# Context handed in turned, layer 3's keys and values computed at the end of the first part, layer 2 quantised by GpSimd, layer 1's scores used in PSUM, and a new order of the queues

## The reference

```
x = x + cross_attention_16_heads(norm(x), ctx)      # layer 0, softmax over the queries
x = x + switch_head_attention(norm(x))              # 8 heads, 5 experts, top 2
x = x + topk_attention(norm(x), ctx, 32)            # layer 1
      scores = (q @ k.T) / sqrt(128); the 32 largest of 77 stay; softmax
x = x + gqa_and_experts(norm(x))                    # causal attention, 8 experts, top 2
x = x + softmax(norm(x) @ ctx.T) @ ctx              # layer 2
x = x + quantised_ffn(norm(x))
      s = sigmoid(clip) * max(abs(n)) / 127         # one scale for the whole tensor
      xq = clip(round(n / s), -128, 127) * s        # 128 -> 352, silu(gate) * up,
      h quantised in the same way, 352 -> 128
x = x + causal_cross_attention_16_heads(norm(x), ctx)   # layer 3
x = x + relu(norm(x) @ w1 + b1) @ w2 + b2
```

## Time and profile before

| | us |
|---|---|
| runs of the kernel before | 1615.16, 1619.88, 1623.08; median 1619.88 |
| profiled execution | 1624.02, its span 1622.1 |
| mean granted TensorE clock of that execution | 0.821 |
| busy: TensorE, VectorE, ScalarE, GpSimd | 1231.1, 1072.0, 989.0, 758.4 |
| part A, up to GpSimd's first all-reduce | about 1245 |
| part B, up to the second all-reduce | about 58 |
| part C | about 319 |

### The profile page before, as it was taken

How to read it: one execution, slowest core, us unless ns; L and a number is a source line. 1 busy time by engine, 2 the same in 40 slices (tenths; PEclk the granted TensorE clock), 3 DMA queues, 4 the chain that set the end, 5 groups by cost and what they waited for, 6 DMA issues and landing times. The chain is left out here.

```text
span 1622.1 us, 36294 instructions
## 1 busy us (share of the span) xinstructions
PE 1231.1 (76%) x13755; PEld 920.0 (57%) x13755; DVE 1072.0 (66%) x2499; ACT 989.0 (61%) x3185; POOL 758.4 (47%) x859
## 2 busy tenths in 40 slices
PE   2677877888787897888888898676752558999986
PEld 2566765675664575566666576454431136777764
DVE  3456665788786677886569777755534879855642
ACT  2677778675768778768768866643432334445531
POOL 2038386485882268458245748732110013433431
PEclk9577677889977897997797988688865569999997
DMA  5000000000000000000000000000001100000000
GB/s 143 1 6 1 1 1 1 2 2 1 4 13 1 16 2 2 6 12 1 1 16 2 1 12 1 1 12 1 1 7 48 47 9 7 12 16 9 9 9 14
DMA packets 29637, 18.26 MB, mean 11 GB/s; under 512 B 6456, under 2 KB 27032, under 8 KB 29464
## 3 DMA queue, kind: packets, MB, share of 16 engines
q1 hardware_dynamic: 29464, 15.93, 3.5%
HBM read 11.73 MB, written 4.19 MB: 10 GB/s over the span
## 5 line engine op out<-in xcount | busy, mean ns | idle before, releaser
L1448 DVE TENSOR_REDUCE arena<-pair 128x8 f32<-128x1024 f32 (+2 forms) x224 | 239.7, 1095 | 115.5 <-PE pair L465 49.5
L1019 ACT ACTIVATE arena<-bank 128x512 f32<-128x512 f32 (+5 forms) x352 | 182.0, 540 | 187.1 <-PE bank L417 86.4
L2073 POOL TENSOR_SCALAR_AFFINE_SELECT arena<-arena 128x1024 f32<-128x1024 f32 (+1 forms) x128 | 145.0, 1154 | 287.8 <-ACT arena L1417 145.7
L2111 POOL TENSOR_TENSOR arena<-arena 128x512 f32<-128x512 f32 x160 | 181.3, 1133 | 50.7 <-DVE arena L1565 35.5
L1079 ACT ACTIVATE arena<-pair,arena 77x128 f32<-77x128 f32 x512 | 178.6, 374 | 23.3 <-DVE arena L1448 22.2
L1027 ACT ACTIVATE arena<-arena 128x128 f32<-128x128 f32 x288 | 117.5, 489 | 105.5 <-POOL arena L2084 97.2
L2116 POOL TENSOR_TENSOR arena<-arena 128x512 f32<-128x512 f32 x128 | 175.1, 1368 | 10.0
L417 PE MATMUL bank<-ident,arena 128*128 128x128 f32 (+2 forms) x448 | 85.6, 327 | 120.0 <-ACT arena L1027 62.5
L417 PEld LDWEIGHTS bank<-ident,arena 128*128 128x128 f32 (+2 forms) x448 | 59.2, 171 | 147.4 <-ACT arena L1027 75.1
L2081 POOL TENSOR_SCALAR arena<-arena 128x4 f32<-128x4 f32 x56 | 18.3, 327 | 225.7 <-DVE arena L1455 223.7
L1417 ACT ACTIVATE arena<-pair 77x1024 f32<-77x1024 f32 x64 | 61.8, 1015 | 99.3 <-PE pair L948 99.3
(11 more groups left out here) (255 smaller groups left out, 3001.9 us busy)
## 6 DMA issues: line engine op xcount, KB each, us to landing
arena<-in_ctx SPq DMA_DIRECT2D x24, 154.0 KB
arena<-in_x SPq DMA_DIRECT2D x8, 256.0 KB, 4.6
spill<-arena SPq DMA_DIRECT2D x8, 256.0 KB, 2.1
arena<-spill SPq DMA_DIRECT2D x8, 256.0 KB, 3.7
out<-arena SPq DMA_DIRECT2D x8, 256.0 KB, 2.5
wexp<-in_L_ffn_expert_w SPq DMA_DIRECT2D x1, 512.0 KB, 4.1
arena<-in_L_ffn_w SPq DMA_DIRECT2D x2, 256.0 KB, 3.1
wsq<-in_L_ffn_Wq SPq DMA_DIRECT2D x1, 256.0 KB, 3.1
```

What stands on the lines that cost most here:

```text
L1019: return act.activation(dst, src, func, bias=bias, scale=scale)
L1448: return dve.tensor_reduce(dst, src, X, op, **kw)
L2073: return pool.affine_select(out=e, in_=e, compare_op=ALU.is_ge, fill=0.0, base=0, pattern=[[0, 8], [1, 128]], channel_multiplier=-1)
L2111: pool.tensor_tensor(into, xvs[:, b, ex * SHD:(ex + 1) * SHD].unsqueeze(1).broadcast_to([128, SH, SHD]), gates[g % 2][:, b, 0:SH, ex].unsq ...
```

## The change

- The host hands the context in a second time, turned (in_ctx_turned, channels first). The transposes and the copies of them are gone in all three places; layer 0 loads only the turned one, layers 1 and 2 both. Each turned tile is loaded when its buffer is free.
- Layer 3's keys and values (stream y, kv3) are computed for all eight groups in part A, from one load of the whole turned context and two weights. That load stands in the SP queue behind the spill of group 5 and waits for the last output of layer 0, whose buffers it takes over. The results stay in SBUF (kf3, v3); part C only spreads them.
- Part B's quantisation is done by GpSimd in the same three passes. The memsets of part C's tiles go to GpSimd behind it. An all-reduce whose result isn't used stands ahead of the first one.
- Layer 1's scores aren't copied: the scale goes into the copy of the queries (with a bias scaled once, b1qs), the first round of the top-k and the exponentials read PSUM, and the bank is drained by the exponentials.
- The last sum is written into x and stored from there; y4 is gone.
- GpSimd's norm waits for the apply of its last use.
- All strings of ORDER are new.

```diff
 ORDER = {
     ("A", "tensor"):
-        "aaaiaaiibbwabwwcbwbcbbcbacaacaabbb...
+        "iiawaaabbwbwwcbbcbbcbacaacabbb...
...
-        "...inlhlkmililkimllmiliimmjnjjjnknnlknnllknnmknnllmllnnmlnnmmnnnnnnnnnnnnnnnn"
+        "...iilliinmlliimilyyymyyymiyyiyyiyynynnyyyjjjnnjknnlknnllnnkmllnknmllnnmlnmmnnnnnnnnnnnnnnn"
     ("A", "scalar"):
-        "aaaaiaibbwwawbcwbbcbb...
+        "iaawaawbbwwbcbbcbbc...
     ("A", "vector"):
-        "awwwawibbwwwcbwabbcbb...
+        "awwiwwwaawbbwwbcbbcbb...
     ("B", "vector"):
-        "aabbabbbbabbbbabbbbabbbbabbbbabbbbbbbbbb",
+        "bbbbbbbbbbbbbbbbbbbbbbbbbbbbbbbb",
+    ("B", "gpsimd"):
+        "aaaaaaaa",
...
             def x0p(g):
                 yield
-                pe.wait_ge(ctx0_in, 16 * (g + 1))
-                o = E.take("x0", g, "ctx")
-                pe.wait_ge(o.drained, o.n)
-                transpose4(o, ctx0[0:CTX], CTX).then_inc(o.full, 1)
-                yield
-                c = E["x0", g, "ctx"]
+                pe.wait_ge(ctx0_in[g % 2], 16 * (g // 2 + 1))
...
             def x1(g):
                 yield
-                pe.wait_ge(ctx_in[g % NCTX], 16 * (g // NCTX + 1))
-                o = E.take("x1", g, "ctx")
-                pe.wait_ge(o.drained, o.n)
-                transpose4(o, ctxg[g % NCTX][0:CTX], CTX).then_inc(o.full, 1)
-                yield
-                c = E["x1", g, "ctx"]
-                pe.wait_ge(c.drained, c.n + 1)
+                pe.wait_ge(ctx_in[g % NCTX], 32 * (g // NCTX + 1))
...
+            def kv3(g):
+                yield
+                if g == 0:
+                    pe.wait_ge(loaded["kv"], NLOAD["kv"])
+                mine = ctxT3[:, g * SEQS * CTX:(g + 1) * SEQS * CTX]
+                o = E.take("kv", g, "k")
+                pe.wait_ge(o.drained, o.n)
+                mm(o.bank[:, 0:SEQS * CTX], w3k[:], mine, start=True, stop=True).then_inc(o.full, 1)
+                yield
+                o = E.take("kv", g, "v")
+                pe.wait_ge(o.drained, o.n)
+                for b in range(SEQS):
+                    ins = mm(o.bank[0:CTX, tokens(b)], mine[:, b * CTX:(b + 1) * CTX], w3v[:], start=True, stop=True)
+                ins.then_inc(o.full, 1)
...
             def x3p(g):
                 yield
-                pe.wait_ge(ctx3_in[g % NX], 16 * (g // NX + 1))
-                o = E.take("x3", g, "ctx")
-                pe.wait_ge(o.drained, o.n)
-                transpose4(o, ctx3[g % NX][0:CTX], CTX).then_inc(o.full, 1)
-                yield
...
                 yield
                 act.wait_ge(x1_max, C.next(x1_max))
-                for b in range(SEQS):
-                    ins = act.activation(p1[:, b, :], sc1[:, b, :], ACT.Exp, bias=neg1[:, b:b + 1])
-                ins.then_inc(C.give(x1_exp), 1)
+                o = E["x1", g, "s"]
+                for b in range(SEQS):
+                    ins = act.activation(p1[:, b, :], o.bank[:, b * CTX:(b + 1) * CTX], ACT.Exp, bias=neg1[:, b:b + 1])
+                ins.then_inc(o.drained, 1)
...
+            def kv3(g):
+                yield
+                o = E["kv", g, "k"]
+                act.wait_ge(o.full, o.n)
+                copy(kf3[:, g, :], o.bank[:, 0:SEQS * CTX]).then_inc(o.drained, 1)
+                yield
+                o = E["kv", g, "v"]
+                act.wait_ge(o.full, o.n)
+                copy(v3[0:CTX, g, :], o.bank[0:CTX, 0:W]).then_inc(o.drained, 1)
...
-                ts(sc1, o.bank[:, 0:SEQS * CTX].rearrange("p (b s) -> p b s", b=SEQS), float(CH) ** -0.5, None, ALU.mult)\
-                    .then_inc(o.drained, 1)
-                dve.wait_ge(o.drained, o.n + 1)
+                scores = o.bank[:, 0:SEQS * CTX].rearrange("p (b s) -> p b s", b=SEQS)
...
             dve.wait_ge(a_done, 4)
-            for each in vdiag3:
-                dve.memset(each, 0.0)
-            dve.memset(nm3, 0.0).then_inc(C.give(dve_step), 1)
-            dve.wait_ge(dve_step, C.last(dve_step))
             dve.wait_ge(gmax_ready, 1)
             act_scale(0)
+            dve.drain().then_inc(ainv_ready, 1)
...
             pool.drain().then_inc(a_done, 1)
+            pool.partition_all_reduce(gmax[:, 3:4], hmax[:, 0:1], 128, bass.bass_isa.ReduceOp.max)
             pool.wait_ge(amax_ready, 1)
             pool.partition_all_reduce(gmax[:, 1:2], gmax[:, 0:1], 128, bass.bass_isa.ReduceOp.max).then_inc(gmax_ready, 1)
+            pool.wait_ge(a_done, 4)
+            pool.wait_ge(ainv_ready, 1)
+
+            def quant2(g):
+                yield
+                pool.wait_ge(xn_in[g % 3], 16 * (g // 3 + 1))
+                if g >= 2:
+                    s = S["b", g - 2, 2]
+                    pool.wait_ge(s.full, s.n)
+                if g:
+                    pool.wait_ge(b_q, g)
+                pool.tensor_scalar(qwork, xn[g % 3], ainv[:, 0:1], ROUND, ALU.mult, ALU.add).then_inc(C.give(pool_step), 1)
+                pool.wait_ge(pool_step, C.last(pool_step))
+                pool.tensor_scalar(qwork, qwork, ROUND + QMAX, ROUND - QMAX - 1.0, ALU.min, ALU.max).then_inc(C.give(pool_step), 1)
+                pool.wait_ge(pool_step, C.last(pool_step))
+                pool.tensor_scalar(xqs[g % 2], qwork, ROUND, None, ALU.subtract).then_inc(C.give(b_q), 1)
+
+            merge(ORDER["B", "gpsimd"], {"a": quant2})
+            for each in vdiag3:
+                pool.memset(each, 0.0)
+            pool.memset(nm3, 0.0)
+            pool.drain().then_inc(c_zeroed, 1)
...
                     sp.dma_start(ctxg[g % NCTX][0:CTX], seqs(d["ctx_1024"], g)).then_inc(ctx_in[g % NCTX], 16)
+                    sp.dma_start(ctxT[g % NCTX], turned(g)).then_inc(ctx_in[g % NCTX], 16)
...
+                if g == 5:
+                    o = E["x0", NG - 1, "o"]
+                    sp.wait_ge(o.drained, o.n + 1)
+                    for dst, src in LOADS["kv"]:
+                        sp.dma_start(dst, src).then_inc(loaded["kv"], 16)
```

236 lines of the change are left out of this document (101 added, 135 removed).

## The result

The changed kernel takes 1661.14 us (median of 4 runs, 1655.36 to 1675.01) against 1621.48 of the kernel before beside it: a ratio of 1.027, with a 95% interval from 1.023 to 1.031. It is 40 us slower; 1608 was forecast, with a range up to 1630.

A forecast was written before the change was run, and what follows sets the result against it. No engine is full mid-first part, where queue order and hand-overs set the time; VectorE, then TensorE bound the third. +5 - 8 + 3.5 - 1 - 11 = -11.5 us gave 1612.5 on the profiled execution, 1608 on the median; range 1588 to 1630.

The forecast's parts named there:

- the third part: End of layer 2 and layer 3: transposes, keys, values and a copy leave the period of 32.37 us; -11 us taken.
- The order in the sum: New queue order: no row prices it; in the first part's middle bounded by about 12 us either way.
- Rival (1): Whole kernel: the new order turns lighter queues to account, about -30 us, hence 1590; chance 0.22.
- Start of part A: Layer 0's work stands behind the late context load: first scores 8.7 us later; +5 us taken, bounds 0 and +8.7.
- Middle of part A: Context transposes, copies and scaling of scores removed per group: -8 us taken, two fifths of the removed work.
- Keys and values at the end of part A: Layer 3's products between layer 1's steps of the last group, mostly covered: +3.5 us, ends 0 and +28.
- Rival (2): Layer 1's chain of group 7: keys and values aren't covered, 28 us at half clock, hence 1633; chance 0.18.
- Part B: Quantised feed-forward: VectorE's period falls from 5.90 to 5.31 us, first quantising on GpSimd not hidden; -1 us, ends -5 and +5.
- the way back to ordinary work: GpSimd after its first all-reduce in the second part: another exchange of code, priced between 0 and 5.95 us.
- the third pass: GpSimd's quantising in the second part: three one-input passes over 512 columns, 0.6 us each, 2.0 together with waits.
- The signs named: Profile after: first scores near 44, second part's period 5.3, GpSimd gap about 6 us, third part about 308 us, period near 31.

The follow-up runs named there:

- e1_c_order_back: The changed kernel with the third part's four order strings put back to those of before, letters of removed steps taken out: 1642.64 us, ratio 1.013.
- e15: The changed kernel with layer 3's keys and values back in the third part, and first and third parts in the old order: 1617.03 us, ratio 1.000.
- e16: As e15, with the second part's quantising also put back on VectorE: 1616.87 us, ratio 0.998.
- e17: As e16, with the feed-forward products of groups 2 to 5 of the third part moved as in e12_gaps_filled: 1611.22 us, ratio 0.994.
- e12_gaps_filled: As e1_c_order_back, with the third part's feed-forward products moved so each of four places before the max scores has 2.3 us or more: 1635.49 us, ratio 1.011.

## Why the prediction was wrong

**The step that failed** is the third part. It said that the values' 1.04 us stand in the middle of a full queue and are gained "for certain", that transposes and keys at worst lengthen the idle times behind them, and took -11 with ends -8 and -18. No end lay above zero. Measured were +36: about 25 for the order, 7 to 9 for the missing products, the rest not settled. Two things were left out. First, the period of 32.4 us was read as TensorE's work, while the queue meets ScalarE's exponentials four times per group; what stands between is not load but cover. The earlier trace rows held the sign of it, 1.22 us of waiting at one of the four places. Secondly, a longer idle time can do more than swallow the gain: behind most of the waits of 1.7 to 1.9 us for the norm the clock fell in e1_c_order_back, and the same matmuls took 2.00 us instead of 1.11. That the steps in front of a wait "only lengthen these" idle times was wrong; the sum had no term for what follows them.

**The order in the sum.** The new order was counted at nothing in part C, and bounded by 12 us either way in part A. Rival (1) had it gain. It cost 18 us in the medians in part C (1659 to 1661 with it, 1642.64 without) and 16.5 in part A where keys and values weren't there; where they were, part A's order doesn't show in the medians (1642.64 and 1640.01).

**Start of part A**: +7.1 measured (42.41 against 35.35), 8.7 was worked out. Right in mechanism and size; what is left of it at the end isn't shown.

**Middle of part A**: -8. e15 and e16, the same removed work in the old order, ended part A 10.3 and 8.8 us before the first all-reduce of the earlier trace rows, e17 4.7. That fits, but isn't shown: it is one profile of before against three, the kernel before was itself 4 us above its median in that profile, and the median of e16 shows only 2.6 for the whole kernel. In the new order it didn't come.

**Keys and values at the end of part A**: +3.5, ends 0 and +28. In the old order 7 to 8.5, counted from the sixth spill; in the new one that stretch was 3 to 7.5 us shorter with them than without. The end below zero was missing here too; a clock of 0.91 with them against 0.69 without points the same way as in part C. Rival (2) named this place as the danger; the kernel with that order and these products shows 1242 to 1257, near the kernel before. It was the slower case, but not by its mechanism.

**Part B**: -1 forecast, +1.6 measured, inside its ends. The period of 5.3 us came as forecast and gave -3.5. Mis-sized were the way back to ordinary work, 8.04 us instead of 5.95, in which GpSimd's inputs weren't counted (about 1.7 us at the most), and the third pass, 1.5 us instead of 0.6: together 3 us. The Trainium skill, "GPSIMD Engine Reference", section 2.1, names about 6 us for the first call of a freshly loaded kernel; the rows show 6.17 into the all-reduce, which agrees, and 8.04 out of it. Its section 4.1 calls one-input work roughly line-rate: true of the two passes that write f32 (0.61 to 0.69), not of the one that writes bf16 (1.49 to 1.52).

**The signs named** for it: the first scores near 44 (42.41), the end of part A about where it was and B's period came. The gap on GpSimd came too, at 8.04 us instead of about 6, and two of its three passes were near 0.6. The third part was to be about 308 us long with a period near 31; it is 355.0 long, and the period, for which staying at 32.4 was named as a sign of being wrong, rose to 36.

The sum after the fact, in the profiles: -5.0 (A) + 1.6 (B) + 36.0 (C) = 32.6, the difference of the two spans. The medians differ by 39.7; the 7 us between are probably the scatter of part A, whose end in this profile was one of the two earliest of nine.

## What to carry to other kernels

Before pricing work that is removed from an in-order queue, write down what stands between each release and the wait that needs it, and compare it with the time of the engine waited for: work in such a place is cover, and taking it out gains nothing until the order is made anew. Count the clock as a term of its own, with an end on the losing side, wherever a removal makes an idle time of TensorE longer, and look at all of its idle times: filling one moved the fall to the next. And test a new order apart from the new code: here the code alone cost 20 us (1640.01), its order another 21, and a few products per group moved by the reading of the trace gained about 5. And when a part's end scatters between profiles, count from a mark inside it that stands just ahead of the change: the end of part A scattered by 15 us, the stretch from the sixth spill by 5.

## What the runs showed of the hardware that was not expected

- TensorE was granted 0.58 and 0.56 for two stretches of 2 us behind an idle time of 1.91 us, in a part where it was busy 159 of 180 us; 32 matmuls took 2.00 us instead of 1.11. Behind the same wait in e12_gaps_filled, 1.93 us, it was granted 1.00.
- Behind waits of 1.74 us the clock fell in some groups and not in others of one kernel: in the changed one 1.00 at 1448 and 0.60 and 0.54 from 1484.
- A queue with 14 us of useless products in it was 7 to 9 us faster than the same queue without them (part C 321.5 us, and 328.6 and 330.3).
- GpSimd stood empty on both sides of the all-reduce: 6.17 us into it, and 8.04 us from it to ordinary work, of which its inputs explain about 1.7 at the most. Twelve profiles with GpSimd's quantising show 7.2 to 9.5 us on the way back.
- A GpSimd pass over 512 columns takes 0.61 to 0.69 us with f32 output and 1.49 to 1.52 with bf16 output. The passes differ in their operation too, and no run holds the two apart.
- The same queues of the first part ended between 1242.0 and 1256.7 us in nine profiles.
